# A mixture-of-experts stage as one program over four batches, weights laid out by expert and split under the first units, gated product kept in PSUM

## Chip, cores and metric

The kernel runs on one core of a Trainium2 chip. The metric is the device time of one execution in microseconds (us); lower is better. A core has five engines with queues of their own: TensorE (PE in the profile; PEld is its weight load), VectorE (DVE), ScalarE (ACT), GpSimd (POOL) and SyncE (SP, which issues the DMAs here). They meet only at semaphores.

## What is computed

A decoder layer over 4 batches of 512 tokens with 512 features, in float32: differential attention, a selective scan (d_state 16) that takes the place of cross attention, and a mixture of experts, each followed by a layer norm. Only the last part matters here:

```python
x2 = layernorm(x1 + scan_output)            # x1 = layernorm(x + attention)
shared = x2 @ sw1.T * sqrelu(x2 @ swg.T) @ sw2.T          # hidden 256
xl = x2 @ Wdown.T                                         # latent 128
probas = sigmoid(x2 @ Wg.T)                               # 16 experts, top 8 by probas + biases
p = top-8 probas / their sum * 2.5                        # 0 for the others
for e in range(16):
    ye = xl @ rw1[e].T * sqrelu(xl @ rwg[e].T) @ rw2[e].T # hidden 256
    acc = acc + p[:, e:e + 1] * ye
out = layernorm(x2 + shared + acc @ Wup.T)
```

All experts are computed for all tokens, weighted with p, which is 0 where an expert isn't chosen.

## The kernel before

Every float32 matrix product is made of three: each operand is split into a high part (rounded to the PE format) and a low part (the remainder), and `three()` (L1319) issues high x high, high x low and low x high into one PSUM bank. So each activation needs a copy to the high part (ScalarE) and a subtraction for the low part (VectorE); the weights are split once (`cw`, a pair of resident tensors of 16448 columns).

`layer()` runs setup, scan inputs, attention with scan, and `expert_phase()`, which is all that changes. Its weights lie in `cw` kind by kind: router, shared, latent down and up, then all rw1, all rwg, all rw2.

*Prologue* (L1444 to L1498, one block). SP loads the residual `acc` of batch 0 into x1, y into yg and the weights in chunks of 1024 columns into three staging areas; ScalarE makes the high parts (L1477), GpSimd the low parts (L1490), and between these the `PREPARE` pieces of batch 0 run one after the other: x0 (add out bias, GpSimd), stats, var, guess (ScalarE Ln and Exp), newton and norm (layer norm 1), tanh, yx and gmul (gate y with silu(x1); the "gating product"), turn (PE transposes gated y, VectorE adds it), layer norm 2, x2T (PE transposes x2, split), gate (router logits and exponential). The last four chunks are left to batch 0.

*Batches.* `experts(b, finish)` is written out for batch 0 and once more as the body of a hardware loop over batches 1 to 3, each a block with a barrier and the clearing of semaphores behind it (L1769). A batch is 34 units: 2 of the shared expert (hidden halves), 32 of the routed ones (expert, hidden half). For unit n: PE makes two up products, G (the relu side) and U, into psGU[n % 3] (two banks, three deep); ScalarE relu (L1641) and square (L1644) into act_buf; GpSimd weights it with the routing weights wb (L1694, routed units); VectorE multiplies it with U into act_buf (L1747, prod); ScalarE copies the high part (L1654) and VectorE subtracts for the low part hid_lo (L1730); PE adds the down product of unit n - 3 into psA (`LAG` = 3). The order in each queue is written out by hand: ScalarE relu_square(n), high(n-1); VectorE prod(n), low(n-1). up(n) waits for the product of unit n-3, relu(n) for hid_lo(n-3).

The pieces of the next batch's preparation are placed at units by `PREPARE` (L1181 to L1204), also in the last batch, where `(b + 1) & (B - 1)` prepares batch 0 again. Routing weights go through DRAM (`wT`) and are broadcast by SP to wb. At the end of a batch the latent sum is split (L1683, L1763), four output products go to psGU and are added to x3; the next batch's block starts with the routing chain on VectorE, the last layer norm of x3 (`last_norm`) and the stores. After the loop a block of its own does this for batch 3.

## Time and profile before

| what | value |
|---|---|
| median of 3 runs | 1919.01 us (1917.92 to 1921.06) |
| profiled execution, its own time | 1916.34 us |
| its span, first to last instruction | 1914.6 us |
| mean granted TensorE clock | 0.897 |
| PE / DVE / ACT / POOL busy | 76% / 74% / 55% / 66% of the span |
| expert stage with its prologue | from about 1325 us to the end |

How to read it: times of rows are microseconds from the start of the span unless marked ns. PE clock is the granted share of full speed (2.4 GHz); 0.5 is 1.2 GHz. In a timeline a number in brackets is the idle time of the engine just before the instruction, and behind the arrow stands what ended it. Durations of matmuls overlap each other, so their spacing is read from their starts.

### The profile page before, as it was taken

How to read it: one execution, taken by the hardware profiler on the slowest of the kernel's cores; microseconds unless marked ns; L12 is line 12 of the kernel's file. 1: busy time of each engine (PE TensorE's matmuls, PEld its weight loads, DVE VectorE, ACT ScalarE, POOL GpSimd, SP SyncE). 2: the span in 40 equal slices, each digit the busy share in tenths (PEclk: the TensorE clock that was granted, in tenths of full speed). 3: DMA queues.
4: the chain of work that ended last, by engine and by line, in shares of the span. 5: the costliest groups of instructions: out<-in, count | busy, mean ns of one | idle time of the engine just before them, and what ended most of it. 6: DMA issues, size and time to landing. Idle time of an engine off the chain costs nothing. (4 is left out here: it accounts for less than half of the span.)

```text
span 1914.6 us, 23797 instructions
## 1 busy us (share of the span) xinstructions
PE 1464.3 (76%) x7680; PEld 1158.5 (61%) x7680; DVE 1410.7 (74%) x2438; ACT 1055.7 (55%) x2413; POOL 1254.9 (66%) x602
## 2 busy tenths in 40 slices
PE   2334206899998999989999979994287887778786
PEld 1111005788777887877888868873155665556564
DVE  3745542788997889978889788884638768677586
ACT  2543332666665666655666656663436547466374
POOL 1221121799997999979999799996736346264262
PEclk9666557899998999998999989998589999999999
DMA  4335443234444343463344523323431121111211
GB/s 129 116 129 185 180 148 117 93 116 126 138 129 158 111 128 93 149 191 102 98 123 144 193 82 112 116 78 115 138 102 48 39 84 47 63 60 33 94 44 38
DMA packets 125442, 210.12 MB, mean 110 GB/s; under 512 B 11204, under 2 KB 60872, under 8 KB 123160
## 3 DMA queue, kind: packets, MB, share of 16 engines
q1 hardware_dynamic: 125336, 208.81, 34.2%
q8 instruction: 54, 0.88, 0.2%
q14 instruction: 52, 0.43, 0.1%
HBM read 158.05 MB, written 50.72 MB: 109 GB/s over the span
## 5 line engine op out<-in xcount | busy, mean ns | idle before, releaser
L1168 POOL TENSOR_TENSOR state<-state,Cn 128x1024 f32<-128x1024 f32 x128 | 311.6, 2434 | 59.4 <-DVE state L1084 59.4
L1174 POOL TENSOR_TENSOR y_sb<-y_sb,state 128x1024 f32<-128x1024 f32 x128 | 307.2, 2400 | 44.1 <-DMA y_sb<-scratch_y 34.0
L1157 POOL TENSOR_TENSOR state<-dtu_sb,Bn 128x1024 f32<-128x1024 f32 x128 | 314.3, 2456 | 31.5 <-DMA Bn<-scratch_bc 17.4
L1084 DVE TENSOR_TENSOR_SCAN state<-dA,state 128x512 f32<-128x512 f32 x256 | 310.3, 1212 | 16.4 <-POOL state L1157 13.5
L1694 POOL TENSOR_TENSOR act_buf<-act_buf,wb 128x512 f32<-128x512 f32 x128 | 179.9, 1405 | 215.9 <-ACT act_buf L1644 215.4
L924 ACT ACTIVATE dA<-dt_sb,negA 128x512 f32<-128x512 f32 x256 | 177.4, 693 | 124.4 <-DVE state L1084 123.7
L553 PE MATMUL psP<-x_hi,w_hi 128*128 128x512 f32 (+1 forms) x512 | 189.0, 369 | 69.7 <-DVE w_lo L988 50.5
L554 PE MATMUL psP<-x_lo,w_hi 128*128 128x512 f32 (+1 forms) x512 | 179.0, 350 | 0.0
L555 PE MATMUL psP<-x_hi,w_lo 128*128 128x512 f32 (+1 forms) x512 | 178.3, 348 | 0.0
L1747 DVE TENSOR_TENSOR act_buf<-psGU,act_buf 128x512 f32<-128x512 f32 x136 | 93.2, 686 | 94.4 <-POOL act_buf L1694 79.4
L1641 ACT ACTIVATE act_buf<-psGU 128x512 f32<-128x512 f32 x136 | 81.1, 596 | 140.1 <-PE psGU L1323 120.3
L553 PEld LDWEIGHTS psP<-x_hi,w_hi 128*128 128x128 f32 x512 | 101.6, 198 | 90.7 <-issue 52.5
L1730 DVE TENSOR_TENSOR hid_lo<-act_buf,hid_hi 128x512 fp32r<-128x512 f32 x136 | 126.5, 933 | 0.6
L1024 DVE TENSOR_REDUCE negmax<-psS 128x2 f32<-128x512 f32 (+3 forms) x128 | 103.5, 809 | 20.6 <-PE psS L754 20.4
L553 PE MATMUL psO<-ow_hi,hT_hi 128*128 128x512 f32 x256 | 108.9, 426 | 11.5 <-DVE ow_lo L993 10.1
L555 PEld LDWEIGHTS psP<-x_hi,w_lo 128*128 128x128 f32 x512 | 101.4, 198 | 12.1
L554 PEld LDWEIGHTS psP<-x_lo,w_hi 128*128 128x128 f32 x512 | 101.9, 199 | 9.2
L1321 PE MATMUL psGU<-xl_hi,cw_hi 128*128 128x512 f32 x256 | 100.8, 394 | 6.0 <-DVE xl_lo L1736 6.0
L555 PE MATMUL psO<-ow_hi,hT_lo 128*128 128x512 f32 x256 | 103.5, 404 | 0.0
L554 PE MATMUL psO<-ow_lo,hT_hi 128*128 128x512 f32 x256 | 103.2, 403 | 0.0
L1323 PE MATMUL psGU<-xl_hi,cw_lo 128*128 128x512 f32 x256 | 100.7, 394 | 0.0
L1322 PE MATMUL psGU<-xl_lo,cw_hi 128*128 128x512 f32 x256 | 100.2, 391 | 0.0
(220 smaller groups left out, 4501.9 us busy)
## 6 DMA issues: line engine op xcount, KB each, us to landing
Bn<-scratch_bc SPq DMA_DIRECT2D x64, 256.0 KB, 4.1
x_hi<-scratch_xs SPq DMA_DIRECT2D x32, 512.0 KB, 4.9
x_lo<-scratch_xs SPq DMA_DIRECT2D x32, 512.0 KB, 5.9
Cn<-scratch_bc SPq DMA_DIRECT2D x64, 256.0 KB, 3.4
scratch_acc<-acc_sb SPq DMA_DIRECT2D x64, 256.0 KB, 2.2
wb<-scratch_wT SPq DMA_DIRECT2D x64, 256.0 KB, 3.3
acc_sb<-scratch_acc SPq DMA_DIRECT2D x48, 256.0 KB, 3.1
w_stage<-in_w SPq DMA_DIRECT2D x32, 256.0 KB, 3.3
```

The lines of the kernel that those rows point to most:

```text
L553: nc.tensor.matmul(out, at_l(lhs[0]), at_r(rhs[0]), start=start, stop=False)
L554: nc.tensor.matmul(out, at_l(lhs[0]), at_r(rhs[1]), start=False, stop=False)
L555: return nc.tensor.matmul(out, at_l(lhs[1]), at_r(rhs[0]), start=False, stop=stop)
L924: nc.scalar.activation(dA[:, :], dt[:, ct, :], ACT.Exp, scale=s["negA"][:, ct * NS + state:ct * NS + state + 1]) \
L1024: nc.vector.reduce_max(negmax[:, u % 2, :], psS[:, u % 2, :, 0:width(u)], AX.X, negate=True) \
L1084: nc.vector.tensor_tensor_scan(row, dA[:, :], row, 0.0, ALU.mult, ALU.add) \
L1157: nc.gpsimd.tensor_tensor(st[:, k % 4], dtu[:, 2 * h:2 * h + 2, :], Bn[:, state % NB, :].unsqueeze(1).broadcast_to([P, 2, T]), ALU.mult).t ...
L1168: nc.gpsimd.tensor_tensor(st[:, k % 4], st[:, k % 4], Cn[:, state % NB, :].unsqueeze(1).broadcast_to([P, 2, T]), ALU.mult).then_inc(S["gat ...
L1174: nc.gpsimd.tensor_tensor(y[:, 2 * h:2 * h + 2, :], y[:, 2 * h:2 * h + 2, :], st[:, k % 4], ALU.add).then_inc(S["piece_done"], 1)
L1321: nc.tensor.matmul(out, at_l(lhs[0]), at_r(rhs[0]), start=start, stop=False)
L1694: nc.gpsimd.tensor_tensor(act_[:, n % 3, :], act_[:, n % 3, :], wb[:, e % 3, :], ALU.mult) \
L1730: nc.vector.tensor_tensor(hid[1][:, n % 3, :], act_[:, n % 3, :], f32(hid[0][:, n % 3, :]), ALU.subtract).then_inc(S["hid_lo"], 1)
```

## The change

- One block, written out for all four batches without a hardware loop, barriers or cleared semaphores between them; semaphores count on through the batches. VectorE routes batch b+1 while the last down products of batch b run; the latent sum of batch b is split in unit 2 of batch b+1, its output products follow units 4 to 7, last_norm lies in units 8 to 11 and the stores behind. Two buffers X[0] and X[1] take turns instead of x1 and x3.
- PREPARE is packed into units 13 to 33 and left out in the last batch. var and guess now share a unit (16, 27), newton and all norms too (17, 28).
- psGU becomes psG (two banks, a ring used in turn by G products, latent, shared down and output products) and psU (four banks). The product is written back into psU, the high copy and the low subtraction read it there. Order on VectorE: low(n-1), prod(n). relu(n) waits for prod(n-3), U(n) for hid_lo(n-4).
- Weights of an expert lie side by side (rw1, rwg, rw2: 768 columns, a chunk). Five chunks of 832 columns and the experts 0 to 4 are split in the prologue, the other eleven in units 0 to 9 of batch 0, five staging slots.
- Prologue: loads in the order x (first half), out bias, x, y, router bias; GpSimd does one split, the four yx, then nine splits; turns use two banks, x2T transposes go tile by tile into the four psU banks.

```diff
 PREPARE = {
-    3: (("x0", 0, 0),),
...
-    9: (("stats", 1, 3), ("var", 1, 0)),
-    10: (("guess", 1, 0), ("newton", 1, 0), ("norm", 1, 0), ("norm", 1, 1)),
-    11: (("norm", 1, 2), ("norm", 1, 3)),
-    12: (("tanh", 0, 0), ("tanh", 0, 1), ("yx", 0, 0), ("gmul", 0, 0)),
...
+    13: (("x0", 0, 0), ("x0", 0, 1)),
+    14: (("x0", 0, 2), ("stats", 1, 0)),
+    15: (("x0", 0, 3), ("stats", 1, 1), ("stats", 1, 2)),
+    16: (("stats", 1, 3), ("var", 1, 0), ("guess", 1, 0)),
+    17: (("newton", 1, 0), ("norm", 1, 0), ("norm", 1, 1), ("norm", 1, 2), ("norm", 1, 3)),
+    18: (("tanh", 0, 0), ("yx", 0, 0)),
+    19: (("tanh", 0, 1), ("yx", 0, 1), ("gmul", 0, 0)),
+    20: (("tanh", 0, 2), ("yx", 0, 2), ("gmul", 0, 1)),
+    21: (("tanh", 0, 3), ("yx", 0, 3), ("gmul", 0, 2)),
+    22: (("gmul", 0, 3),),
+    23: (("turn", 0, 0),),
+    24: (("turn", 0, 1), ("stats", 2, 0)),
+    25: (("turn", 0, 2), ("stats", 2, 1)),
+    26: (("turn", 0, 3), ("stats", 2, 2)),
+    27: (("stats", 2, 3), ("var", 2, 0), ("guess", 2, 0)),
+    28: (("newton", 2, 0), ("norm", 2, 0), ("norm", 2, 1), ("norm", 2, 2), ("norm", 2, 3)),
+    29: (("x2T", 0, 0),),
...
     33: (("gate", 0, 0),),
-    34: (("gate", 0, 1),),
 }
...
+BASE, EXPERT = 832, 768
+CHUNKS = [(BASE * n, BASE * (n + 1)) for n in range(5)] + [(RW + EXPERT * e, RW + EXPERT * (e + 1)) for e in range(NE)]
+NCH = len(CHUNKS)
...
+EARLY = 10
+SPLIT_AT = {0: (10,), 1: (11, 12)}
+SPLIT_AT.update({n: (n + 11,) for n in range(2, 10)})
...
-        psGU = ps("psGU", [P, 3, 2, T])
+        lat = [m[:, 0, :] for m in x2T]
+        psG = ps("psG", [P, 2, T])
+        psU = ps("psU", [P, 4, T])
...
-                    def low(n):
-                        dve.wait_ge(S["hid_hi"], n + 1)
-                        nc.vector.tensor_tensor(hid[1][:, n % 3, :], act_[:, n % 3, :], f32(hid[0][:, n % 3, :]),
-                                                ALU.subtract).then_inc(S["hid_lo"], 1)
+                def low(b, n):
+                    N = NU * b + n
+                    dve.wait_ge(S["hid_hi"], N + 1)
+                    nc.vector.tensor_tensor(hid[1][:, N % 3, :], psU[:, N % 4, :], f32(hid[0][:, N % 3, :]),
+                                            ALU.subtract).then_inc(S["hid_lo"], 1)
+
+                def prod(b, n):
+                    N = NU * b + n
+                    dve.wait_ge(S["up_done"], N + 1)
+                    if n < 2:
+                        dve.wait_ge(S["square_done"], N + 1)
+                    else:
+                        dve.wait_ge(S["weighted"], routed(b, n) + 1)
+                    nc.vector.tensor_tensor(psU[:, N % 4, :], psU[:, N % 4, :], act_[:, N % 3, :], ALU.mult) \
+                        .then_inc(S["prod_done"], 1)
...
-        experts(0, False)
-        with nc.Fori(0, B - 1) as b:
-            experts(b + 1, True)
```

The order of PE's queue and of SP's around the x loads, new:

```diff
+                for b in range(B):
+                    for n in range(NU):
+                        if n == 2:
+                            pe.wait_ge(S["xl_lo"], b + 1)
+                        up(b, n)
+                        if n == 0:
+                            if b > 0:
+                                down(b - 1, NU - 3)
+                                down(b - 1, NU - 2)
+                            turn_weights(b)
+                            latent(b)
+                            if b > 0:
+                                down(b - 1, NU - 1)
+                        if n in (2, 3):
+                            shared(b, 2 * n - 4)
+                            shared(b, 2 * n - 3)
+                        if 4 <= n < 8 and b > 0:
+                            output(b - 1, n - 4)
+                        for piece in PREPARE.get(n, ()) if b + 1 < B else ():
+                            prepare_pe(pe, b + 1, *piece)
+                        if n - LAG >= 2:
+                            down(b, n - LAG)
...
+                        if e == 6:
+                            if b > 0:
+                                store_out(sp, b - 1)
+                            if b + 1 < B:
+                                if b > 0:
+                                    sp.wait_ge(S["stored"], 16 * TT * b)
+                                else:
+                                    sp.wait_ge(S["cw_lo"], NCH)
+                                for h in range(2):
+                                    load_x(sp, b + 1, h)
```

## Rows read from the trace of the kernel before

**Rows 1.** Busy time by stretch: start:end, length, PE, PEld, DVE, ACT, POOL (count), PEclk, DMA.

```profile
1318.00:1394.00 76.00, 17.52 (x64) 10.16 (x65) 34.00 (x47) 23.60 (x32) 44.15 (x22) 0.57 0.44 142
1394.00:1523.80 129.80, 104.51 (x436) 78.65 (x436) 87.36 (x143) 73.94 (x127) 64.28 (x44) 0.96 0.19 62
1523.80:1652.00 128.20, 103.23 (x436) 77.66 (x436) 92.34 (x159) 71.58 (x125) 56.54 (x40) 0.97 0.19 58
1652.00:1778.30 126.30, 101.59 (x436) 76.43 (x436) 92.11 (x158) 71.25 (x125) 56.46 (x40) 0.99 0.18 59
1778.30:1898.00 119.70, 98.49 (x424) 74.25 (x424) 88.77 (x153) 70.72 (x123) 56.52 (x40) 0.99 0.19 62
1898.00:1914.60 16.60, 3.03 (x12) 2.18 (x12) 9.53 (x21) 1.00 (x3) 0.00 (x0) 0.75 0.17 63
```

**Rows 2.** Timeline, first up product of batch 0 and last latent copy: start, length, instruction.

```profile
1394.01 0.61 PE L1321 MATMUL psGU<-x2T_hi,cw_hi 128*128 128x512 f32 x1 [1.25 <-PEq L89]
...
1898.01 0.59 ACT L1683 CAST xl_hi<-psA 128x512 fp32r<-128x512 f32 x1 [1.68 <-PE psA L1323]
```

**Rows 3.** Timeline of PE at full clock: spacing of matmuls and of four transposes.

```profile
1397.96 0.40 PE L1322 MATMUL psGU<-x2T_lo,cw_hi 128*128 128x512 f32 x1
...
1400.99 0.40 PE L1323 MATMUL psGU<-x2T_hi,cw_lo 128*128 128x512 f32 x1
...
1599.93 0.60 PE L1333 MATMUL psM<-ident,yg 128*128 128x128 f32 x4
1600.28 0.47 PE L1321 MATMUL psA<-hid_hi,cw_hi 128*128 128x512 f32 x1
```

**Rows 4.** Waits of PE, 1523.8 to 1652.0: whom for, us, times, longest.

```profile
PE psA L1321 <- DVE hid_lo L1730: 13.7, 12, 2.0
PE psM L1321 <- DVE hid_lo L1730: 3.6, 1, 3.6
...
PE psM L1333 <- DVE x L1424: 0.7, 1, 0.7
```

**Rows 5.** Timeline, relu, weighting and product of one routed unit.

```profile
1600.12 0.60 ACT L1641 ACTIVATE act_buf<-psGU 128x512 f32<-128x512 f32 x1 [0.63 <-PE psGU L1323]
...
1601.47 1.36 POOL L1694 TENSOR_TENSOR act_buf<-act_buf,wb 128x512 f32<-128x512 f32 x1 [1.12 <-ACT act_buf L1644]
...
1602.87 0.69 DVE L1747 TENSOR_TENSOR act_buf<-psGU,act_buf 128x512 f32<-128x512 f32 x1 [0.59 <-POOL act_buf L1694]
```

**Rows 6.** Timeline of the prologue: x0, last gating product, a split, the router.

```profile
1337.36 4.92 POOL L1434 TENSOR_TENSOR x<-x,outb 128x512 f32<-128x512 f32 x4 [17.71 <-DMA x<-scratch_acc]
...
1359.11 2.74 DVE L1420 SCALAR_TENSOR_TENSOR yg<-gate,yg 128x512 f32<-128x512 f32 x1 [1.22 <-POOL yg L1439]
...
1379.47 2.35 POOL L1490 TENSOR_TENSOR cw_lo<-x,cw_hi 128x1024 fp32r<-128x1024 f32 x1 [4.01 <-ACT cw_hi L1477]
...
1387.05 0.59 PE L1321 MATMUL psM<-x2T_hi,cw_hi 128*16 128x512 f32 x1 [1.49 <-DVE x2T_lo L1428]
```

**Rows 7.** DMA issues, 1325 to 1400: size, us from issue to landing.

```profile
yg<-scratch_y SPq DMA_DIRECT2D x1, 1024.0 KB, 9.2
...
rbias<-in_route_b SPq DMA_DIRECT2D x1, 8.0 KB, 5.6
```

**Rows 8.** Single lines: min/median/max ns of low, product, and a ScalarE form in PSUM.

```profile
L1730 DVE TENSOR_TENSOR hid_lo<-act_buf,hid_hi x136: 673/683/2439, 1409.3 to 1896.1; 128x512 fp32r<-128x512 f32 x136
...
L1747 DVE TENSOR_TENSOR act_buf<-psGU,act_buf x136: 673/690/693, 1402.7 to 1894.7; 128x512 f32<-128x512 f32 x136
...
L870 ACT ACTIVATE psS<-psS,negmax x128: 326/491/654, 341.8 to 1304.9; 128x256 f32<-128x256 f32 x32, 128x384 f32<-128x384 f32 x32, 128x128 f32<-128x128 f32 x32, 128x512 f32<-128x512 f32 x32
```

**Rows 9.** Single lines of the preparation: min/median/max ns of norm and table load.

```profile
L1404 DVE TENSOR_SCALAR x<-x,mv,rstd x56: 532/541/2570, 1344.6 to 1910.9; 128x512 f32<-128x512 f32 x56
...
L1376 ACT ACT_TABLE_LOAD  x5: 1283/1283/1283, 1344.9 to 1833.0; - x5
```

**Rows 10.** DMA issues, 1520 to 1650: size, us to landing.

```profile
out<-x SPq DMA_DIRECT2D x4, 256.0 KB, 4.2
x<-scratch_acc SPq DMA_DIRECT2D x2, 512.0 KB, 3.8
```

More of the change, by code:

```diff
@@ L1407, in prepare_dve @@
-        def prepare_dve(dve, step, kind, i, n, before=0):
+        def prepare_dve(dve, step, b, kind, i, n):
+            x = X[b % 2]
             if kind == "stats":
-                tile_stats(dve, step, x1, n, S["x0_done" if i == 1 else "x2_added"])
+                dve.wait_ge(S["x0_done" if i == 1 else "x2_added"], TT * b + n + 1)
+                step(nc.vector.bn_stats(stats[:, n, :], x[:, n, :]))
+                step(nc.vector.bn_aggr(mv[:, n, :], stats[:, n, :]))
             elif kind == "var":
-                variance(dve)
+                nc.vector.tensor_scalar(var[:, :], mv[:, :, 1], EPS, None, ALU.add).then_inc(S["var_done"], 1)
@@ L1412, in prepare_dve @@
             elif kind == "newton":
[L1413 removed]
+                dve.wait_ge(S["guess_done"], 2 * b + i)
+                rsqrt_newton(nc.vector, step, rstd[:, :], var[:, :], tmp[:, :])
             elif kind == "norm":
[L1415 removed]
+                nc.vector.tensor_scalar(x[:, n, :], x[:, n, :], mv[:, n, 0:1], rstd[:, n:n + 1],
+                                        ALU.subtract, ALU.mult).then_inc(S["norm_done" if i == 1 else "x2_done"], 1)
@@ new lines, in expert_phase @@
+        for b in range(B + 1):
+            if b < B:
+                gring += [("up", b, 0), ("xl", b, 0), ("up", b, 1), ("up", b, 2), ("sh", b, 0), ("sh", b, 1),
+                          ("up", b, 3), ("sh", b, 2), ("sh", b, 3)]
+                for n in range(4, NU):
+                    gring += [("up", b, n)]
+                    gring += [("out", b - 1, n - 4)] if b > 0 and n < 8 else []
+            else:
+                gring += [("out", B - 1, t) for t in range(TT)]
+        G_AT = {user: i for i, user in enumerate(gring)}
@@ L1444, in expert_phase, with routed, store_out @@
+        def routed(b, n):
+            return (NU - 2) * b + n - 2
+        def store_out(sp, b):
+            for t in range(TT):
+                sp.wait_ge(S["out_done"], TT * b + t + 1)
+                sp.dma_start(d["out"].rearrange("(b t p) n -> b t p n", b=B, p=P)[b, t], X[b % 2][:, t, :]) \
+                    .then_inc(S["stored"], 16)
         with nc.Block() as block:
@@ new lines, in output, with turn_weights @@
+                def output(b, t):
+                    wait_gbank(pe, "out", b, t)
+                    pe.wait_ge(S["lat_lo"], b + 1)
+                    three(gbank("out", b, t), lat, cw, lambda a: a[:, t * P:(t + 1) * P],
+                          lambda a: a[:, WUP:WUP + HID], True, True).then_inc(S["out_ps"], 1)
+                def turn_weights(b):
+                    pe.wait_ge(S["route_done"], b + 1)
+                    for t in range(TT):
+                        mm = nc.tensor.transpose(psM[0:NE, t * P:(t + 1) * P], sel[:, t, :], s["ident"][:, :])
+                    mm.then_inc(S["wT_ps"], 1)
@@ L1466, in _ @@
+                for n in range(NU - LAG, NU):
+                    down(B - 1, n)
+                for t in range(TT):
+                    output(B - 1, t)
             @block.scalar
             def _(act):
-                nc.scalar.preload_act_table_set("natural_log_exp_and_others")
-                PAUSE = 8
-                mine = [p for p in pieces if p[0] in ("guess", "tanh", "x2T", "gate")]
-                for n, (a, z) in enumerate(chunks):
-                    if n < 5 or n >= PAUSE:
-                        for piece in mine[n if n < 5 else n - PAUSE + 5:][:1]:
-                            prepare_act(act, *piece)
-                    act.wait_ge(w_load[n % NST], 16 * (n // NST + 1))
-                    nc.scalar.copy(cw[0][:, a:z], staged(n)).then_inc(w_hi, 1)
@@ L1789, in layer @@
+                low(B - 1, NU - 1)
+                lat_low(B - 1)
+                for t in range(TT):
+                    add_out(B - 1, t)
+                for t in range(TT):
+                    last_norm(B - 1, t)
 def layer(nc, d):
```

718 lines of the change are left out of this document (350 added, 368 removed).

## Prediction

> **What bounds the kernel now.** Only the last stage is touched, so the first thing to read is its table by stretch [rows 1]. Columns to look at are PE busy and the granted clock. A batch of the expert stage lasts 126 to 130 us, PE is busy 101 to 104 us of it, no other engine more than 92 us. Ahead of the batches lies the stretch 1318 to 1394 with 17.5 us of PE work in 76. Second, the ends of this stage [rows 2]: the first up product starts at 1394.0, and the last latent copy at 1898.0; the stretches of [rows 1] are cut at the first up product of each batch and at that copy, with 16.6 us left behind it.
>
> What PE must do in one batch follows from its instruction spacing. Between 1397.96 and 1400.99 lie 13 matmul starts of 512 columns, 0.233 us each [rows 3]. A batch has 396 of them (shared up 48, experts up 192 and down 96, shared down 24, latent 12, output 12, router 12): 92.3 us. Nine groups of four transposes take 0.35 each (1599.93 to 1600.28) [rows 3]: 3.2. Together **95.5 us**. The remaining 31 us per batch are in the view of who waited for whom [rows 4]: 24.3 us of waits (13.7 for hid_lo ahead of a down product, 3.6 ahead of the shared down product, 1.5 for each latent split, 1.9 for the barrier, 2.1 for transposes); the rest is lower granted clock after long waits (0.96 and 0.97 in the first two batches, 0.57 in the stretch ahead of them [rows 1]) and pipeline tails. The first and last of the seven kinds of waits stand in rows 4.
>
> So the kernel is a PE pipeline held up by its vector chain. One routed unit of that chain [rows 5]: from relu over square to the GpSimd weighting 1.35 us, to the product 1.40, then the product (0.69 [rows 8]) and, with 0.03 for the signal, the high copy; some 0.5 to 0.6 later ScalarE can take its next relu. Since ScalarE queues high(n-1) behind relu(n), this loop covers two units: 4.0 us, **2.0 us a unit**, against 9 x 0.233 = 2.1 us of PE. There is next to no reserve: what the preparation of the next batch adds to ScalarE, VectorE or GpSimd shows up on PE once the lag of three units (reserve about 1.6 us) is used.
>
> **The change part by part.**
>
> *Prologue.* Before, the weight splits go through GpSimd between the pieces of batch 0 (13 splits of 1024 columns here, the rest in batch 0): the last gating product ends only at 1361.9, 2.7 us long instead of 0.7 because the split beside it holds it, and the router starts at 1387.05 [rows 6]. After, one split comes first, then the four yx together, and nine more splits follow (832 or 768 columns, 1.9 or 1.8 us scaled from the 2.35 us of 1024 [rows 6]). But rbias is now queued behind both x loads and y, and GpSimd waits for it: y landed 9.2 us after its issue at 1331.9, rbias 5.6 us after 1330.3 [rows 7]; so x0 starts near 1341 instead of 1337.4 (bounds: no delay, 3.7). From 1341: four x0 4.9, stats, guess and newton 2.3 (1348.2), four norms and yx at 1.7 each against the lock (1355.6), last gating product behind one split (1359 to 1360). From there to the router it took 25.2 us; now turns with two banks 7.6 (VectorE's add, stats and aggregate, 1.6, four times, and one turn), guess and norms 5 as before, transposes per tile into four open banks 4.3: 16.9. Then the router as before, 1387.05 to 1394.0, without the barrier's 1.3: 5.7. The first up product starts near **1382.5, 11.5 us earlier** (bounds 6 and 16).
>
> *Splits beside units 0 to 9 of batch 0.* Each adds about 0.8 us to ScalarE and 1.8 to GpSimd; GpSimd then needs 1.3 + 1.8 = 3.1 us a unit over eight units, 25 us, against PE's 22.4 (which has the shared down product there): +4 us (0 to 8).
>
> *Barriers, latent and output tail.* Up of the next batch covers the last down products, the latent copy and the output; the latent for the experts is covered by up(1). Of the 24.3 us of waits the barrier, both latent waits and most of the 3.6 go, and so does the slow first unit. New waits at the head: sh(0) for hid_lo(1) 0.7, up(3) for shared_added through the two-bank ring 1.2, up(4) 0.6, out(1) for x3_done 1.4, and about 1 in units 5 to 7, where VectorE has low, product, add and stats (2.75 us) against PE's 2.8. I take 5 us a batch.
>
> *Subtraction from PSUM.* hid_lo reads PSUM and one SBUF tile. Before it took 0.68 alone and up to 2.4 beside GpSimd, mean 0.93; instructions with their tensor in PSUM stay within 0.67 to 0.69 [rows 8]. So some 0.25 x 34 = 8.5 us of VectorE per batch go; on PE's path it is perhaps 2 to 3, and it is in the delays below. The order low(n-1), product(n) makes a second loop: product 0.72, high 0.62, low 0.60 = 1.94 us a unit, under PE's 2.1. The product written into PSUM has no VectorE row; the nearest is the product with the same PSUM input written to SBUF, 0.69, and I take that; ScalarE in the attention stage reads and writes PSUM in at most 0.65 [rows 8].
> By the Trainium skill ("VectorE: DVE Perf Modes", the section on the TRN2 errata) a VectorE instruction on PSUM has a fixed part 62 cycles longer than one on SBUF, 65 ns more for each subtraction; rows 8 show 17 ns between the two minima, and either would leave that loop below 2.1 us.
>
> *Preparation of the next batch, moved and packed.* Before it is spread from unit 3 to 34; after it lies in 13 to 33. I followed the chain unit by unit with the durations of [rows 5, 8, 9], counting from relu(12) = 0 with PE alone giving 2.1 us a unit. x0 in 13 to 15 (four times 1.3 on GpSimd): weighting of 14 is 1.7 late, of 16 2.7. stats and var of unit 16 come behind product(16), and ScalarE waits with guess in that same unit: relu(17) at 16.5 instead of 10.5. newton and four norms in 17, then the table load and a tanh behind relu(18): relu(19) at 22.4 instead of 14.7. A tanh, a yx and a gating product in each of 19 to 21 and the second table load (1.28 [rows 9]): relu(22) at 31.7 instead of 21.0. Then PE itself waits: turn(0) in unit 23 needs the gating product of 22, so the up product of 24 is done at 37.6 instead of 25.2: **12.3 us lost**. From 24 on PE leads again. In 27 var and guess share a unit once more (2.9), in 28 come newton and four norms, and the first x2T in 29 needs all of them: PE gets there 2.8 after relu(28) could start and can go on at 9 to 11, **7 us lost**. The two long waits also drop the clock, 1 us each. Sum 21 us per batch with preparation, where before it was 13.7 + 2.1.
>
> *x of the next batch.* Two x buffers mean that batch b+1 loads into the buffer from which b-1 is stored. The last norm is in unit 11; product and norm 3.9, the last store 2.1 (half of the 4.2 that four queued ones take), load 3.8 [rows 10]: x arrives some 10 us after relu(11), 12 with the whole 4.2; GpSimd wants it at 6.9. +3 us in batches 1 and 2 (0 to 8: wb of expert 7 is queued on SP behind the store wait and both loads).
>
> *Last batch.* It no longer prepares a batch that nobody uses: 6 us of PE (12 router matmuls and eight groups of transposes, 2.8 each, and four small ones) and all the waits that it makes.
>
> **The sum** (against the profiled execution: span 1914.6, its time 1916.3, the median of the three runs 2.7 above that).
> Batch 0: 95.5 - 2.8 (no output) + 1.6 (slow first unit) + 3 (head) + 4 (splits) + 21 = 122.3, before 129.8.
> Batches 1 and 2: 95.5 + 5 + 21 + 3 = 124.5 each, before 128.2 and 126.3.
> Batch 3 to the latent copy: 393 matmuls (9 carried over) 91.6 + 0.4 + 5 + 1 + 2.2 (down(33) waits for its split) = 100.2, before 119.7.
> Ending: add and stats alternate (4 x 1.65), no barrier: 15.4, before 16.6 [rows 1].
> 1382.5 + 122.3 + 249.0 + 100.2 + 15.4 = 1869.4; with 1.7 around the span and 2.7 to the median **1874 us**, 2.3% faster. Of the 45 us, 19.5 come from the last batch without its preparation, 11.5 from the prologue, 7.5 from batch 0, 5.5 from batches 1 and 2 together, 1.2 from the ending.
>
> **The rivals.**
> A. *The preparation hides better* than my chain says: its waits cost what they did before (13.7 + 2.1), as VectorE is freed of the port wait. For: the DVE busy column falls by 8 us. Against: guess in the unit of var, and PE waiting directly behind norms and gating product. 3 x 9 us less: 1847.
> B. *It hides worse*: norms and gating products (VectorE, all tensors in SBUF) were stretched up to 2.6 and 2.7 us beside GpSimd [rows 6, 9], and with the lows out of the way they are now the ones that collide, 10 us more per batch: 1904.
> C. *The product in PSUM is slower* (the other side). If reading and writing PSUM costs x more than 0.69, the second loop is 1.94 + x. Over 0.16 it exceeds PE's 2.1 and costs x - 0.16 in each of some 100 units that nothing else delays. At x = 0.6 that is 44 us and the gain is gone: above 1919, say 1930. Against: PSUM input costs nothing visible, and the ScalarE row.
> D. *The prologue doesn't get shorter*, as rbias and the splits hold GpSimd: 1885. That is the step "it overlaps the weights" not happening.
>
> **How the numbers follow.** Forecast with its own range 1858 to 1892: 0.53. A 0.20, B 0.17, C 0.05, D 0.05. The range takes in A and B with the bounds of the prologue and of x: 1836 to 1906. A measurement of this kernel can tell about 0.2%, 4 us. Slower needs C, or B with a delay three times as large: 0.05; same 0.03; faster 0.92.
>
> **What would show it.** Prologue: first x2T up product near 1382, x0 later than 1337, the first turn before 1361. Batches: starts 122 to 125 apart with one PE wait of 4 to 6 us ahead of the first turn and one ahead of the first x2T in three batches, and none in the fourth, which is near 100. hid_lo mean near 0.69. A product mean above 0.85 would be C. I am wrong if batches 1 and 2 are much shorter than 124 (the chain was counted too dear) or the last one isn't much shorter than the others.

## The result, and the profile after

In comparison on one chip the changed kernel takes 1896.6 us (median of four runs, 1891.1 to 1900.0), the kernel before 1918.5 (median of four): ratio 0.989, interval 0.987 to 0.992. It is 22 us faster, where 45 were forecast (1874 us, range 1858 to 1892): faster, as forecast, but outside the range. The profiled execution took 1891.14 us, with a span of 1889.3.

First the stretches of the expert stage, in the columns of [rows 1]. The first begins at the issue of the first load of x, the others at the first up product of each batch, and the last at the high copy of the last latent.

```profile
1324.12:1376.73 52.61, 12.04 (x48) 7.87 (x48) 27.83 (x44) 16.30 (x24) 27.13 (x16) 0.55 0.41 131
1376.73:1507.33 130.60, 101.67 (x418) 75.80 (x416) 74.58 (x134) 76.94 (x132) 75.17 (x53) 0.93 0.26 79
1507.33:1640.69 133.36, 106.42 (x438) 80.50 (x436) 86.24 (x158) 68.90 (x124) 51.80 (x40) 0.92 0.17 56
1640.69:1773.86 133.17, 107.41 (x439) 81.03 (x437) 86.25 (x158) 68.90 (x124) 51.82 (x40) 0.92 0.17 56
1773.86:1873.14 99.28, 93.25 (x399) 73.21 (x397) 65.91 (x117) 61.56 (x110) 41.44 (x32) 1.00 0.17 54
1873.14:1889.30 16.16, 5.55 (x12) 3.61 (x12) 9.54 (x21) 0.99 (x3) 0.00 (x0) 0.61 0.18 65
```

The same cuts in the kernel before, for the prologue and for the last batch with its ending:

```profile
1330.89:1394.01 63.12, 13.85 (x49) 7.58 (x49) 32.50 (x44) 22.07 (x31) 42.49 (x21) 0.53 0.46 146
...
1778.33:1914.60 136.27, 101.52 (x436) 76.43 (x436) 98.30 (x174) 71.69 (x126) 56.52 (x40) 0.96 0.19 62
```

| stretch | before | forecast | after | after against before | against forecast |
|---|---|---|---|---|---|
| prologue, from the load of x | 63.1 | 51.6 | 52.6 | -10.5 | +1.0 |
| batch 0 | 129.8 | 122.3 | 130.6 | +0.8 | +8.3 |
| batch 1 | 128.2 | 124.5 | 133.4 | +5.2 | +8.9 |
| batch 2 | 126.3 | 124.5 | 133.2 | +6.9 | +8.7 |
| batch 3 and ending | 136.3 | 115.6 | 115.4 | -20.8 | -0.2 |

(1382.5 less 1330.9 is the 51.6.) The stage is 18.5 us shorter. The profiles of the two kernels differ by 25 us, since in this execution the stage also began 6.8 us earlier; that is no effect of the change. Over the thirteen profiles of this study the first load of x is issued anywhere from 1323.1 to 1335.6 us behind the same instructions. So stretches are compared from here on, not spans.

The prologue, the last batch and the ending came out as forecast. What failed is every batch that prepares the next one: they were to become shorter, and became longer. The clock column says the same from another side: 0.92 and 0.93 in those three, 1.00 in the one that prepares nothing. Who waited for whom in batch 1, on TensorE (us in total, times, longest), against [rows 4]:

```profile
PE psA L1313 <- DVE hid_lo L1768: 8.5, 4, 4.6
PE psM L1343 <- DVE x L1406: 6.7, 1, 6.7
PE psM L1333 <- DVE yg L1412: 5.0, 1, 5.0
PE psG L1313 <- DVE x L1792: 1.9, 2, 1.3
PE psG L1313 <- ACT act_buf L1631: 1.6, 1, 1.6
```

Twelve short waits for hid_lo have become four long ones. With the rest these waits make 26.9 us.

### The profile page after: what moved, and what is told of

It reads as the page before. It is cut to its first block and busy times, and to the rows that moved or that the text cites. A ratio compares the mean times of both kernels' runs of the same rounds, so it can differ in the third digit from the quotient of the medians.

```text
span 1889.3 us, 23507 instructions
## 1 busy us (share of the span) xinstructions
PE 1460.0 (77%) x7632; PEld 1155.9 (61%) x7632; DVE 1356.7 (72%) x2394; ACT 1036.3 (55%) x2397; POOL 1227.2 (65%) x598
## 5 line engine op out<-in xcount | busy, mean ns | idle before, releaser
L1732 POOL TENSOR_TENSOR act_buf<-act_buf,wb 128x512 f32<-128x512 f32 x128 | 167.1, 1306 | 251.4 <-ACT act_buf L1633 251.4
L1768 DVE TENSOR_TENSOR hid_lo<-psU,hid_hi 128x512 fp32r<-128x512 f32 x136 | 93.8, 690 | 116.2 <-ACT hid_hi L1645 115.5
L551 PEld LDWEIGHTS psP<-x_hi,w_hi 128*128 128x128 f32 x512 | 101.2, 198 | 91.6 <-issue 52.6
L1778 DVE TENSOR_TENSOR psU<-psU,act_buf 128x512 f32<-128x512 f32 x136 | 94.4, 694 | 53.4 <-POOL act_buf L1732 34.6
L1631 ACT ACTIVATE act_buf<-psG 128x512 f32<-128x512 f32 x136 | 81.4, 599 | 89.2 <-PE psG L1315 89.2
L1645 ACT CAST hid_hi<-psU 128x512 fp32r<-128x512 f32 x136 | 79.0, 581 | 52.7 <-DVE psU L1778 52.1
L868 ACT ACTIVATE prob<-psS,negmax 128x256 f32<-128x256 f32 (+3 forms) x128 | 67.3, 526 | 63.3 <-DVE negmax L1022 61.6
L551 PE MATMUL psS<-kT_hi,qT_hi 128*128 128x256 f32 (+3 forms) x256 | 96.3, 376 | 0.0
```

The source lines that it names most:

```text
L551: nc.tensor.matmul(out, at_l(lhs[0]), at_r(rhs[0]), start=start, stop=False)
L1732: nc.gpsimd.tensor_tensor(act_[:, N % 3, :], act_[:, N % 3, :], wb[:, E % 3, :], ALU.mult) \
L1768: nc.vector.tensor_tensor(hid[1][:, N % 3, :], psU[:, N % 4, :], f32(hid[0][:, N % 3, :]), ALU.subtract).then_inc(S["hid_lo"], 1)
L1778: nc.vector.tensor_tensor(psU[:, N % 4, :], psU[:, N % 4, :], act_[:, N % 3, :], ALU.mult) \
```

## The experiments

**What the dropped preparation of a fifth batch is worth.** The kernel before, with its last batch written out with an empty table of preparation pieces.

```diff
-        with nc.Fori(0, B - 1) as b:
+        with nc.Fori(0, B - 2) as b:
             experts(b + 1, True)
+        experts(B - 1, True, {})
```

> The kernel before, with its loop over two batches and the last batch written out without the preparation of a fifth batch (which the kernel before computes and throws away); all else as before, barriers included. Theory (most of what the change gained is this dropped work, the rest was given back to the clock): the last batch is 18 to 20 us shorter and the whole 17 to 22 us faster than before (about 1899). Rival (the gain came from the barriers that fell away and the product in PSUM): the last batch shrinks by under 10 us.

Ratio to before 0.993, interval 0.991 to 0.996. Its last batch with the ending:

```profile
1777.57:1903.30 125.73, 96.94 (x388) 72.79 (x388) 73.13 (x130) 64.42 (x110) 44.98 (x32) 0.93 0.16 51
```

10.6 us less than 136.3, not 18 to 20, and also not under 10: neither side is right, and the whole is 12.9 us faster (1903.0 against 1915.9), not 17 to 22. In the kernel before, a preparation costs 10.6 us, give or take some 3: batch 2 of this run, with the same code as batch 2 of the kernel before, took 129.5 us where that one took 126.3. In the changed kernel the batches with and without it differ by 133.2 - 99.3 = 34 us (the last batch also does its own last three down products, which the others leave to the next). The new layout makes a batch without preparation much cheaper, 115.4 against 125.7 with the ending, and a preparation three times as dear.

**Is the low clock what makes it dear?** Extra matmuls into psM, their product thrown away, ahead of the four longest waits (so many per unit), so that TensorE rests for a shorter time.

```diff
+WARM = {17: 14, 20: 11, 23: 18, 29: 24}
...
+                        if b + 1 < B and n in WARM:
+                            keep_warm(b, WARM[n], n > 26)
                         for piece in PREPARE.get(n, ()) if b + 1 < B else ():
                             prepare_pe(pe, b + 1, *piece)
```

> The kernel after, with 14, 11, 18 and 24 extra matmuls of 128x512 (product thrown away) put ahead of the preparation's pieces or the down products at which TensorE waits longest (units 17, 20, 23 and 29 of batches 0 to 2), so that it is busy through the waits. Theory (each long wait of TensorE lets its clock fall and the matmuls behind it run at half the rate, some 2 us for each of four waits): a batch with a preparation is 6 to 8 us shorter, its granted clock 0.97 or more, the whole some 20 us less than after (about 1872). Rival (VectorE and ScalarE bound these stretches, so what TensorE regains is waited for again at the next tile): under 5 us in all, and the waits elsewhere grow by what the clock gives back. If the extra matmuls reach past the waits, the batch is longer by what they overhang, 0.22 us each.

Batches 0 and 1:

```profile
1382.46:1511.14 128.68, 112.31 (x484) 85.03 (x482) 74.57 (x134) 76.93 (x132) 75.37 (x53) 0.99 0.25 80
1511.14:1641.56 130.42, 115.79 (x505) 87.80 (x503) 86.24 (x158) 68.94 (x124) 52.15 (x40) 1.00 0.16 57
```

The mean clock of the three batches is back at 0.99, 1.00 and 0.99, and they are 1.9, 2.9 and 1.3 us shorter, 6.2 in all: neither the 6 to 8 a batch of the theory, nor quite the rival's under 5. The timeline of TensorE in batch 1 shows where the rest went, after and then with the extra matmuls:

```profile
1573.11 0.79 PE L1313 MATMUL psA<-hid_hi,cw_hi 128*128 128x512 f32 x1 [4.64 <-DVE hid_lo L1768]
1573.70 0.63 PE L1314 MATMUL psA<-hid_lo,cw_hi 128*128 128x512 f32 x1
```

```profile
1576.99 0.50 PE L1314 MATMUL psA<-hid_hi,cw_hi 128*128 128x512 f32 x1 [1.50 <-DVE hid_lo L1778]
...
1580.40 0.50 PE L1314 MATMUL psA<-hid_hi,cw_hi 128*128 128x512 f32 x1 [1.07 <-DVE hid_lo L1778]
...
1582.97 0.51 PE L1314 MATMUL psG<-xl_hi,cw_hi 128*128 128x512 f32 x1 [1.61 <-ACT act_buf L1641]
```

Counted from the start of the batch the wait ends at 65.8 in both kernels. The 1.3 us that the full clock saves behind it appear as a new wait of 1.07, and at the following up product (71.8 in both) nothing is left. Only behind the first turn and the first x2T transposes does it stay in this batch: relu(24) comes 1.5 us earlier against relu(12), and the next batch 2.9 earlier. In batches 0 and 2 the rest of 2.3 us that the extra matmuls left ahead of the first turn was followed by a fall of the clock soon after its end. The 3 us from the first turn on, in batches 0, 1 and 2:

```profile
1471.65:1474.65 3.00, 3.00 (x11) 2.47 (x12) 1.84 (x3) 0.04 (x1) 0.00 (x0) 0.65 0.30 87
1603.52:1606.50 2.98, 2.98 (x18) 2.54 (x18) 1.84 (x3) 0.86 (x2) 0.00 (x0) 1.00 0.26 88
1733.90:1737.00 3.10, 3.08 (x12) 2.56 (x13) 1.86 (x3) 0.57 (x1) 0.00 (x0) 0.73 0.32 85
```

From the first turn to the first x2T it took 0.4, 1.6 and 0.0 us less than in the changed kernel, so that batch 1 alone shows the full gain. By the Trainium skill ("TensorE: Matmul & The Clock Gate", the section on HAM oscillation) matmuls on the low clock cost wall time in the measure of their extra length; that gives the spacing seen here, and where the vector chain is the bound, as behind 1573.11, the trace disagrees that it is all wall time.

**Two steps of the variance in one unit.** The guess one unit behind the variance, in units 16 and 17 and likewise in 27 and 28.

```diff
-    16: (("stats", 1, 3), ("var", 1, 0), ("guess", 1, 0)),
-    17: (("newton", 1, 0), ("norm", 1, 0), ("norm", 1, 1), ("norm", 1, 2), ("norm", 1, 3)),
+    16: (("stats", 1, 3), ("var", 1, 0)),
+    17: (("guess", 1, 0), ("newton", 1, 0), ("norm", 1, 0), ("norm", 1, 1), ("norm", 1, 2), ("norm", 1, 3)),
```

> The kernel after, with the first Newton guess of the second and third preparation step moved one unit later than the variance it needs (units 17 and 28 in place of 16 and 27). Theory (the 3.4 us wait of the down product in unit 20, and its stretch at the low clock, come from two steps of the variance chain in one unit): one long wait and some 1.5 us of low clock less in each prepared batch, 3 to 5 us a batch, 9 to 15 us in all. Rival (VectorE's total work in units 17 to 20 sets it, wherever the step stands): within 2 us a batch.

```profile
1375.80:1503.80 128.00, 103.82 (x418) 78.18 (x416) 74.99 (x134) 77.17 (x132) 75.14 (x53) 0.91 0.26 81
1503.80:1633.41 129.61, 108.11 (x438) 82.47 (x436) 86.57 (x158) 69.15 (x124) 51.95 (x40) 0.91 0.18 57
```

2.6, 3.8 and 3.5 us shorter, 9.8 in all, at the low end of the 9 to 15 expected; ratio to before 0.984, interval 0.981 to 0.988. The granted clock did not rise (0.91), though less time at the low clock had been expected: in batch 1 TensorE waits 21.5 us instead of 26.9 and works 108.1 instead of 106.4. So this gain is from the chain and not from the clock. ScalarE waited inside unit 16 for a variance that VectorE makes last in it, with relu(17) queued behind.

**The late x.** Last norms two a unit, to start stores and the load two units earlier.

```diff
-                        if 8 <= n < 12 and b > 0:
-                            last_norm(b - 1, n - 8)
+                        if n in (8, 9) and b > 0:
+                            last_norm(b - 1, 2 * n - 16)
+                            last_norm(b - 1, 2 * n - 15)
```

> The kernel after, with the last norm of the batch before done two rows' tiles per unit in units 8 and 9 in place of one in each of units 8 to 11, so that its stores and the load of the next batch's input start two units (about 8 us) earlier. Theory (GpSimd's 3.3 us wait for that input in unit 16, batches 1 and 2, is what makes the down product of unit 17 wait 4.6 us): this wait goes, with its 1.3 us of low clock, some 5 us in each of batches 1 and 2, about 10 us in all; units 8 and 9 lose 1 to 2 us to the denser work. Rival (the product of unit 17 waits for VectorE anyway, as in batch 0 where no input is late): under 2 us.

Batches 1 and 2 took 132.8 and 130.1 us, 0.6 and 3.1 less; ratio 0.987, interval 0.983 to 0.990, as after. SyncE reaches the stores only behind a load of wb that waits for weightings, so they began 47.5 us into batch 1 as before, and the load of x was issued at 55.2 instead of 56.0 (53.2 in batch 2). GpSimd's wait for x fell from 3.3 to 2.7 us in batch 1 and from 3.2 to 0.7 in batch 2: the batches shrank by about what that wait shrank. So the link from late x to the length of the batch is as the theory has it, with 3 us and not 5 to be had a batch, and the edit reached it in one batch of two.

**Is it the packing?** Two kernels, one execution each, in which the output (sum, statistics, norm) is formed in a scratch tile, so that x and y of the next batch can be loaded at expert 2. They leave out the residual, and the stores move another tile of the same size in place of the output, so that they take the time of the work but do not give the layer's result. The first spreads the preparation of batches 1 and 2 as the kernel before did (units 3 to 33), the second keeps the packed table.

```diff
+                        if e == 2 and 0 < b < B - 1:
+                            sp.wait_ge(S["shared_added"], TT * b)
+                            for h in range(2):
+                                load_x(sp, b + 1, h)
...
-                        for piece in PREPARE.get(n, ()) if b + 1 < B else ():
+                        for piece in (SPREAD if b else PREPARE).get(n, ()) if b + 1 < B else ():
```

> The kernel after, with two edits. The output of a batch (sum, statistics, norm) is formed in a scratch tile of its own instead of in the x buffer, with the same instructions, so that x of batch b+2 can be loaded at expert 2 of batch b+1 (this leaves the residual out of the output, so the result is another). And batches 1 and 2 prepare the next batch by the table of the kernel before, spread over units 3 to 33. Batch 0 keeps the packed table. Theory (the preparation costs 31 us a batch only because it is packed into units 13 to 33 behind one another; each step waits for the one before): batches 1 and 2 take 112 to 118 us in place of 133, with TensorE waiting under 13 us in each. Rival (the sum of vector work bounds the batch, however it is spread): 127 or more.

> The control for the kernel with the spread table: the same scratch tile for the output (residual left out) and the same early load of x, but the packed table in all batches. Theory (of the 133 us, the late x of the next batch is 3): batches 1 and 2 take 130 to 131 us, batch 0 and 3 as in after. Rival (the scratch tile or the early load itself changes the batches): outside 128 to 134.

Batches 1 and 2, spread, then packed:

```profile
1506.99:1627.57 120.58, 105.53 (x438) 78.69 (x436) 84.95 (x158) 68.69 (x124) 51.90 (x40) 0.96 0.20 62
1627.57:1748.25 120.68, 104.62 (x439) 78.60 (x437) 84.95 (x158) 68.55 (x124) 51.90 (x40) 0.96 0.20 62
```

```profile
1516.17:1646.18 130.01, 105.10 (x438) 79.39 (x437) 86.23 (x158) 68.91 (x124) 51.94 (x40) 0.93 0.17 57
1646.18:1775.98 129.80, 104.77 (x438) 79.22 (x437) 86.20 (x158) 68.92 (x124) 51.96 (x40) 0.93 0.18 58
```

The control gives the late x: 133.3 - 129.9 = 3.4 us a batch. The spread table gives another 9.3, and TensorE's waits in batch 1 fall from 24.9 to 14.8 us. With the same instructions on every engine, and the same busy time on VectorE within 1.3 us, the batch is 9.3 us shorter: so the sum of vector work is not the bound, and the places in the order are. It is less than the theory wanted: 120.6 us against 112 to 118, with waits of 14.8 against under 13. This table was made for the other kernel and has crowded units of its own: relu(13) comes 7.5 us behind relu(12), where 2.7 is usual.

**The product in PSUM.** Product, high copy and subtraction back on a tile in SBUF. Since that tile stays in use until the subtraction has read it, relu(n) must again wait for hid_lo(n-3) and not only for the product.

```diff
-                        act.wait_ge(S["prod_done"], N - 2)
+                        act.wait_ge(S["hid_lo"], N - 2)
...
-                    nc.scalar.copy(hid[0][:, N % 3, :], psU[:, N % 4, :]).then_inc(S["hid_hi"], 1)
+                    nc.scalar.copy(hid[0][:, N % 3, :], act_[:, N % 3, :]).then_inc(S["hid_hi"], 1)
...
-                    nc.vector.tensor_tensor(hid[1][:, N % 3, :], psU[:, N % 4, :], f32(hid[0][:, N % 3, :]),
+                    nc.vector.tensor_tensor(hid[1][:, N % 3, :], act_[:, N % 3, :], f32(hid[0][:, N % 3, :]),
...
-                    nc.vector.tensor_tensor(psU[:, N % 4, :], psU[:, N % 4, :], act_[:, N % 3, :], ALU.mult) \
+                    nc.vector.tensor_tensor(act_[:, N % 3, :], psU[:, N % 4, :], act_[:, N % 3, :], ALU.mult) \
```

> The kernel after, with the product, the copy of its high part and the subtraction of the low part on a tile in SBUF, as in the kernel before (undoes the gated product in PSUM). Theory (two SBUF operands let GpSimd hold the subtraction: mean 0.93 instead of 0.69 us, 8 us a batch on VectorE, of which part reaches TensorE): the last batch, without a preparation, is 4 to 8 us longer with more waits for hid_lo, a batch with a preparation 3 to 8 us, 10 to 25 us in all. Rival (the loop has room for it): under 1 us a batch.

1924.1 us, ratio to before 1.0045, interval 1.003 to 1.006: without this part the change would have made the kernel slower. Batch 1 and the last:

```profile
1521.92:1661.82 139.90, 108.74 (x439) 81.50 (x437) 95.21 (x158) 70.22 (x124) 53.42 (x40) 0.90 0.16 53
...
1801.74:1922.20 120.46, 100.58 (x411) 75.22 (x409) 80.68 (x138) 63.52 (x113) 41.77 (x32) 0.95 0.17 53
```

The four batches are longer by 11.0, 6.5, 6.8 and 5.0 us, 29 in all, above the 25 of the expectation. Two lines of VectorE in batch 1 (count, busy, mean ns, idle before), after and then with the tile in SBUF:

```profile
L1768 DVE TENSOR_TENSOR hid_lo<-psU,hid_hi 128x512 fp32r<-128x512 f32 x35 | 24.1, 689 | 32.5 <-ACT hid_hi L1645 32.3
L1778 DVE TENSOR_TENSOR psU<-psU,act_buf 128x512 f32<-128x512 f32 x34 | 23.6, 693 | 14.4 <-POOL act_buf L1732 9.5 <-PE psU L1315 4.9
```

```profile
L1768 DVE TENSOR_TENSOR hid_lo<-act_buf,hid_hi 128x512 fp32r<-128x512 f32 x35 | 33.9, 969 | 33.2 <-ACT hid_hi L1645 33.0
L1778 DVE TENSOR_TENSOR act_buf<-psU,act_buf 128x512 f32<-128x512 f32 x34 | 23.1, 681 | 11.4 <-POOL act_buf L1732 6.5 <-PE psU L1315 4.9
```

The subtraction goes from 689 to 969 ns as both its inputs lie in SBUF, 9.8 us a batch; the product costs 12 ns more in PSUM. What stretches it is the company of GpSimd: of the 136 subtractions of this run 90 overlap a GpSimd instruction and have a mean of 1117 ns, the other 46 one of 689 and at most 695; in the changed kernel both kinds have 690. How much of the 5.0 to 11.0 us a batch is this, and how much the later relu, was not tried apart. The Trainium skill ("SBUF — State Buffer", the section on who interferes with whom) gives as the one meeting point between these engines a port that GpSimd shares with a VectorE instruction with two SBUF inputs; the two means agree with it.

**The splits.** All 21 chunks ahead of the units, none under them.

```diff
-EARLY = 10
-SPLIT_AT = {0: (10,), 1: (11, 12)}
-SPLIT_AT.update({n: (n + 11,) for n in range(2, 10)})
+EARLY = NCH
+SPLIT_AT = {}
```

> The kernel after, with all 21 weight chunks loaded and split ahead of the first up product, none under the units of batch 0. Theory (a split under a unit costs 0.3 to 0.5 us, one in the prologue 1.8 us of GpSimd): the first up product starts 18 to 22 us later against the start of the stage, batch 0 is 3 to 5 us shorter up to unit 12. Rival (the splits under the units are what makes batch 0 as slow as the others): batch 0 shorter by over 8 us.

```profile
1335.64:1387.97 52.33, 11.97 (x49) 7.82 (x49) 27.76 (x44) 16.30 (x24) 27.10 (x16) 0.55 0.44 139
...
1387.97:1525.38 137.41, 105.49 (x418) 79.91 (x416) 78.36 (x134) 77.90 (x132) 75.27 (x53) 0.88 0.24 72
```

I had the place wrong. The first up product needs five chunks and starts as before (52.3 against 52.6); the later chunks queue on ScalarE in front of relu(0), which comes 21.9 us into the batch instead of 3.1, and on GpSimd in front of its first weighting. In this one execution batch 0 is 6.8 us longer. So the splits under the units save 6.8 us against splits in one block. But they are not cheap: from relu(4) to relu(12) batch 0 takes 22.3 us with them and 15.9 in this run, at least 6.4 us for all of them, where the forecast had 4. That batch 3, which has no splits, takes 22.6 for the same units does not speak against it, since it has the output products and last norms there, which batch 0 lacks.

**The router bias.** Loaded ahead of x and y, one execution.

> The kernel after with the small router bias loaded ahead of x in place of behind x and y. Theory (GpSimd's first sum waits for that load alone, which landed 9.5 us after its issue): from the issue of the first x load to the first sum 7.5 to 8.5 us instead of 11.4, and the first up product 3 to 4 us earlier against that issue (49 instead of 52.6). Rival (gating and y set this stretch, y lands 8.6 us after its issue): the first up product within 1 us.

The load of x was issued at 1329.43, and the first sum on GpSimd no longer waits for the bias:

```profile
1335.42 4.92 POOL L1427 TENSOR_TENSOR x<-x,outb 128x512 f32<-128x512 f32 x4 [19.20 <-DMA outb<-in_out_b]
...
1329.43:1377.02 47.59, 12.04 (x48) 7.84 (x49) 27.51 (x44) 15.92 (x24) 27.16 (x16) 0.58 0.46 145
```

6.0 us from load to sum in place of 11.4 (7.5 to 8.5 expected), and the prologue 5.0 us shorter, more than the 3 to 4 expected. Batch 0 grew by 0.9.

**All of it together.** Output formed in the y tile, free until the next y is loaded; x loaded at unit 7; router bias first; two last norms a unit; batches 1 and 2 prepare over units 9 to 33; then, in a second kernel, the down product ahead of the turn and the transposes of its unit.

```diff
+EARLIER = {
+    9: (("x0", 0, 0),),
...
+    13: (("stats", 1, 3), ("var", 1, 0)),
+    14: (("guess", 1, 0), ("newton", 1, 0), ("norm", 1, 0), ("norm", 1, 1)),
...
+    19: (("yx", 0, 3), ("gmul", 0, 2), ("gmul", 0, 3)),
+    21: (("turn", 0, 0),),
...
+    27: (("norm", 2, 2), ("norm", 2, 3)),
+    29: (("x2T", 0, 0),),
...
+                        if e == 5 and b > 0:
+                            if b + 1 < B:
+                                sp.wait_ge(S["x3_done"], TT * b)
+                                for h in range(2):
+                                    load_x(sp, b + 1, h)
+                            store_out(sp, b - 1)
```

> The kernel after, reworked by what the runs showed: the output of batch b-1 is summed and normed in the y tile, which is free until the next y is loaded, so x of the next batch is loaded at unit 7 instead of after the stores; its last norms come two a unit; batches 1 and 2 prepare over units 9 to 33 with a unit between variance and guess, between the last gating product and the first turn and between norms and the first transposes; batch 0 keeps the packed table with guess a unit later and the norms over two units; rbias is loaded first. Theory (each step of the packed table waits for the one before): batches 1 and 2 take 118 to 123 us (after: 133), batch 0 126 to 128, the stage up to the first up product is 3 us shorter, and the whole is 30 to 36 us faster than after (1860 to 1867). Rival (earlier steps collide with the output work of units 4 to 11, where VectorE has low, product, add and stats in every unit): batches 1 and 2 above 126.

> The reworked kernel with TensorE's order changed inside a unit: the down product of three units before comes ahead of the turn or the x2T transposes, not behind them. Theory (TensorE waits at the first turn and the first x2T, and a down product of 0.7 us can be done within that wait): 0.5 to 1.5 us a prepared batch shorter than the reworked kernel. Rival (the vector chain gets its turned tile 0.7 us later in every unit, x2T above all, and pays it back): equal or slower.

The first: 1866.8 us, ratio to before 0.976, interval 0.973 to 0.979. The second: 1863.4 us, ratio 0.973, interval 0.970 to 0.976, which is 2.7% faster than before, against the change's 1.1%. Batches 0 to 3 (the last with its ending) of the second:

```profile
1378.54:1502.61 124.07, 100.67 (x417) 75.14 (x415) 75.48 (x134) 76.62 (x132) 75.04 (x53) 0.94 0.27 83
1502.61:1624.80 122.19, 102.93 (x439) 75.88 (x437) 87.17 (x158) 68.56 (x124) 52.74 (x40) 0.99 0.18 61
1624.80:1746.99 122.19, 102.94 (x438) 75.64 (x436) 87.14 (x158) 68.56 (x124) 52.69 (x40) 0.99 0.20 61
1746.99:1862.20 115.21, 98.05 (x411) 76.25 (x409) 74.30 (x138) 62.63 (x113) 41.75 (x32) 0.95 0.16 55
```

The first had 125.7, 123.7 and 123.5: batch 0 was 0.3 us below its expected range, batches 1 and 2 were 0.5 to 0.7 us above theirs, and the down product in front gave 1.3 to 1.7 us a batch, which decides for its theory (0.5 to 1.5) and against its rival. These kernels change several things at once; what each is worth was not tried apart. VectorE does 0.9 us more in batch 1 than in the changed kernel, and the batch is 11.2 us shorter.

## Why the prediction was wrong in its size

*The batches with a preparation.* The chain was followed unit by unit from relu(12), and this is how it went in batch 0, relu of units 12, 17, 22, 24, 29, 30 and 33:

```profile
1428.57 0.60 ACT L1631 ACTIVATE act_buf<-psG 128x512 f32<-128x512 f32 x1
...
1444.67 0.58 ACT L1631 ACTIVATE act_buf<-psG 128x512 f32<-128x512 f32 x1
...
1460.98 0.60 ACT L1631 ACTIVATE act_buf<-psG 128x512 f32<-128x512 f32 x1
...
1469.53 0.60 ACT L1631 ACTIVATE act_buf<-psG 128x512 f32<-128x512 f32 x1 [4.53 <-PE psG L1315]
...
1484.12 0.60 ACT L1631 ACTIVATE act_buf<-psG 128x512 f32<-128x512 f32 x1
...
1492.86 0.60 ACT L1631 ACTIVATE act_buf<-psG 128x512 f32<-128x512 f32 x1 [1.49 <-PE psG L1315]
...
1502.31 0.60 ACT L1631 ACTIVATE act_buf<-psG 128x512 f32<-128x512 f32 x1 [0.30 <-PE psG L1315]
```

relu(17) at 16.1 (forecast 16.5) and relu(22) at 32.4 (31.7) were right or nearly so (0.7 late). Then it parts:

- *"turn(0) in unit 23 needs the gating product of 22, so the up product of 24 is done at 37.6"*: relu(24), for which the forecast had 37.6, came at 41.0. From the first turn to relu(24) it takes 2.1 us with the clock kept up (batch 1 of the run with extra matmuls) and took 3.7 here: 1.6 for the low clock, where 1 stood in the sum. Of the other 1.8, 0.7 were there at relu(22), and most of the rest is the gating product of unit 22, which has a weighting and a product ahead of it on two engines and itself took 1.47 us, twice its length alone.
- *"the first x2T in 29 ... 7 us lost"*: the wait was 6.7, right, with 1.6 us of low clock behind it where 1 stood in the sum.
- Behind the first x2T three more follow through one bank: each needs the copy and the subtraction of the one before, and the units come 3.15 us apart (1492.86 to 1502.31), where up and down products and transposes of a unit take 2.45 (2.1 and 0.35). That is 2.1 us, the same with the clock kept up. It was missing from the sum.

So the term that failed is the 21 us for the preparation; in batch 0 it was 27 to 29. From relu(12) to the next batch it took 78.8 us. Without a preparation relu(33) comes at 42.5 (batch 3), the next batch could start 1.4 later, and the preparation's own TensorE work is 6.0; the rest is 28.9 (27.3 if the 21 units are counted at the forecast's 2.1 us each; in batch 3 they take 2.02). The three points above are 4.8 us of the 6 to 8 that were missing (2.4 at the first turn, 0.3 at the first x2T, 2.1 behind it); the rest was not taken apart.

*The same error seen from TensorE.* The prediction added TensorE's work at full clock, 95.5, to its waits. In batch 1 its waits came out as forecast: 5 + 21 - 2 + 3 = 27 against 26.9 (the parts less well: 3.9 at the head, 23.0 behind it, so the match is in part luck). The step that failed, on this side, is "The two long waits also drop the clock, 1 us each", with nothing for the tails of the pipeline. The time spent working was 133.4 - 26.9 = 106.5 us, of which the sum allowed 97.5. The prediction had itself found some 7 us of lower clock and pipeline tails in a batch of the kernel before ("the remaining 31", 24.3 of them waits), and carried only 2 of them over. They did not go with the barrier: they stand behind every long wait, and there were four of these. By the spacing of the matmuls in batch 1, about 8.5 us are lost at the low clock (some 5 in the same batch before) and 2.5 in matmuls that drain ahead of a wait; the last batch, with 6 us of waits, loses some 0.4 at the low clock and came out as forecast.

But it would be wrong to call those 8 us the cause. In batch 1 the extra matmuls took the low clock away (1.00) and gave back 2.9 of the 8.9 us by which the forecast was short. The other 6 stay with the clock at 1.00: the vector chain is late by so much in any case, TensorE spends that time waiting or working slowly, and work at full clock plus waits is a sum only where TensorE leads. The cause of the longer batches is the packed order, as the spread table (-9.3) and the guess moved one unit (-3.3 on the mean) show.

*x of the next batch*: forecast +3, measured 3.4 by the control. *Splits*: 4 forecast, at least 6.4 measured, so that 2.4 of the 8.3 us in batch 0 are theirs. *Prologue*: forecast 11.5, measured 10.5 shorter, with the delay of x0 by the router bias as described (11.4 us from the load, where 1341 - 1330.9 = 10.1 were allowed). That the delay costs 5.0, above its upper bound of 3.7, is shown by the run with the bias first.

*Subtraction from PSUM*: mean 689 ns against the 0.69 forecast, so the size per instruction was right, and rival C is out, with the product at 693. (The "17 ns between the two minima" is a misreading of rows 8, where both minima are 673 and the medians 7 ns apart; nothing hung on it.) But "on PE's path it is perhaps 2 to 3" was far too low: undone together with what goes with it, the later relu, it costs 5.0 us even in the batch that prepares nothing, and 6.5 to 11 in the others. It did not raise the error of the sum, since the durations in the chain were those with PSUM.

*Last batch*: 99.3 against 100.2, right. The reason given for it was half wrong: "19.5 come from the last batch without its preparation". The preparation of a fifth batch cost 10.6 in the kernel before. Of the other 10, 5.0 are the product in PSUM, by the run that undoes it; that the rest is the barrier and the latent waits is argued, not shown.

*The rivals.* A is out, and so is D, with the prologue 10.5 us shorter. B, "hides worse", at +10 us a batch lies near what happened (+8.6 on the mean), but not by the mechanism that it named, that norms and gating products collide more than before. In batch 1 the eight norms have a mean of 0.66 us, the four gating products 1.08 and the four last norms 1.13, 14.1 us together; in batch 1 of the kernel before the twelve norms had 0.70 and the gating products 1.23, together 13.3. Against their lengths alone (0.54 and 0.69) the norms and gating products of the preparation cost 2.5 us a batch on VectorE. What part of it reaches TensorE was not tried apart.

## What to carry to other kernels

When work is moved under a pipeline, its price is not only the sum of its instructions; it lies as much in the places where one unit must finish something that the same or the next unit needs. Put a unit between a statistic and its use, and between the last vector step and the transpose that reads it: that, with the earlier x that made room for it, brought the batches from 133 to 122 us with nearly the same instructions. Ask first which buffer forces the work to start late, since here the x buffer, held by an output that another tile could hold, was what packed the table. And price a low clock by what the engine does behind it: it counts in full only where everything else follows TensorE.

## What the runs showed of the hardware

Extra matmuls through the waits kept the mean granted clock of a batch at 0.99 to 1.00 where it had been 0.92 and 0.93, and returned at most 2.9 of the some 8 us that the low clock had taken. The same rest of 2.3 us ahead of the first turn was followed by a clock of 0.65, 1.00 and 0.73 in three batches of one execution. A VectorE subtraction of 128x512 with both inputs in SBUF had a mean of 1117 ns where it overlapped a GpSimd instruction and 689 where it did not; with one input in PSUM it had 690 in both cases. The stages ahead of the experts, the same in all thirteen profiles, varied by 12.5 us from execution to execution, while the last batch with its ending took 115.0 to 116.0 us in each of the ten kernels of the changed layout that kept the product in PSUM.
